# Score buffers and the down-weight quantiser of a transformer layer: one PSUM region for every query tile, and two of the quantiser's passes on ScalarE

## The reference, cut to what matters

```python
def ternary_quant(w):
    scale = jnp.mean(jnp.abs(w)) + EPS
    q = jnp.clip(jnp.round(w / scale), -1.0, 1.0) * scale
    return w + jax.lax.stop_gradient(q - w)

# attention of one head: softmax(q k^T * scale, causal) v
scores = jnp.einsum('bkgtd,bksd->bkgts', qg, k) * scale
scores = jnp.where(causal, scores, -jnp.inf)
attn = jax.nn.softmax(scores, axis=-1)

# feed-forward part, D = 2048, D_EXPERT = 8192
up = jnp.einsum('bsd,ed->bse', x, ternary_quant(W_up))
gate = jnp.einsum('bsd,ed->bse', x, ternary_quant(W_gate))
hidden = jax.nn.silu(up) * gate
out = jnp.einsum('bse,de->bsd', hidden, ternary_quant(W_down))
```

## Time and profile before

| what | us |
|---|---|
| median of 2 runs | 8734.99 |
| the 2 runs | 8610.41 and 8859.57 |
| the profiled execution | 8481.26 |
| its span on the slowest core | 8479.5 |
| its spans on the 8 cores | 8459.3 to 8479.5 |

### The profile page before, as it was taken

How to read it: one execution, slowest core, us unless ns; L and a number is a source line. 1 busy time by engine, 2 the same in 40 slices (tenths; PEclk the granted TensorE clock), 3 DMA queues, 4 the chain that set the end, 5 groups by cost and what they waited for, 6 DMA issues and landing times.

```text
span 8479.5 us, 68560 instructions; the slowest of 8 cores (8459.3 to 8479.5 us)
## 1 busy us (share of the span) xinstructions
PE 4851.5 (57%) x22987; PEld 2208.8 (26%) x22987; DVE 3210.5 (38%) x4854; ACT 1728.5 (20%) x3014; POOL 639.7 (8%) x1086
## 2 busy tenths in 40 slices
PE   1533443444444433346511149999999999587686
PEld 1111111111111111122211124444444444233232
DVE  4044424432444244312365655555555554000000
ACT  3123323332333233211111112112211111000000
POOL 0111111111111111100000000000000000000000
PEclk9855565556555655577755569999999999798898
DMA  2222222222222222242244432122121221424333
GB/s 83 32 76 85 82 43 85 82 74 51 82 77 76 57 75 77 70 100 79 75 129 127 132 114 78 75 76 84 75 77 75 78 81 48 143 85 143 94 83 88
DMA packets 279157, 709.29 MB, mean 84 GB/s; under 512 B 119488, under 2 KB 119520, under 8 KB 246688
## 3 DMA queue, kind: packets, MB, share of 16 engines
q0 software_dynamic: 157216, 350.46, 14.8%
q1 hardware_dynamic: 121600, 354.46, 12.8%
HBM read 607.32 MB, written 109.05 MB: 84 GB/s over the span
## 4 chain that ended last, share of the span: by engine, by line
PE 53%; DVE 14%; DMA 12%; ACT 9%; issue 7%; POOL 2%; another core or an unknown queue 1%; SPq 1%; DVEq 0%; ACTq 0%; POOLq 0%
PE up_ps L1239 11%; PE gt_ps L1253 10%; PE po_a L1340 5%; PE po_b L1340 5%; DMA tdT_scr<-tds 5%; PE a_ps L462 5%; PE y_ps L752 3%; PE pr_ps L879 3%; PE pt_ps L617 3%; DVE stt L660 2%; ACT slabA L1169 2%; PE a_ps L650 2%; DMA xm<-xmid_scr 2%; ACT tds L1084 2%; DVE pt_bf L625 2%
## 5 line engine op out<-in xcount | busy, mean ns | idle before, releaser
L1239 PE MATMUL up_ps<-slabB,slabA 128*128 128x512 bf16 x4096 | 974.2, 399 | 59.7 <-ACT slabA L1169 59.7
L1253 PE MATMUL gt_ps<-slabB,slabA 128*128 128x512 bf16 x4096 | 904.9, 379 | 0.0
L617 PE MATMUL pt_ps<-id_bf,b 128*128 128x128 bf16 x2176 | 292.1, 303 | 848.3 <-DVE stt L687 462.4
L462 PE MATMUL a_ps<-slabA,wcol_bf 128*128 128x512 bf16 x1536 | 389.2, 418 | 313.1 <-DMA wcol_bf<-Wq 164.4
L1239 PEld LDWEIGHTS up_ps<-slabB,slabA 128*128 128x128 bf16 x4096 | 412.8, 102 | 590.3 <-issue 162.2
L1253 PEld LDWEIGHTS gt_ps<-slabB,slabA 128*128 128x128 bf16 x4096 | 401.0, 98 | 483.1
L700 ACT ACTIVATE w<-a_ps,stt 128x1024 f32<-128x1024 f32 (+7 forms) x384 | 329.3, 861 | 909.5 <-DVE stt L687 668.5
L1078 PE MATMUL tp_ps<-id_bf,b 128*128 128x128 bf16 x1024 | 139.6, 303 | 636.6 <-DMA tdT_scr<-tds 477.3
L650 PE MATMUL a_ps<-k_bf,q_bf 128*128 128x512 bf16 (+3 forms) x640 | 259.2, 526 | 386.9 <-DVE q_bf L565 248.0
L401 ACT ACTIVATE pdump<-pw 128x1024 f32<-128x1024 f32 x384 | 404.2, 1054 | 370.1 <-DMA pw<-W_down 125.8
L617 PEld LDWEIGHTS pt_ps<-id_bf,b 128*128 128x128 bf16 x2176 | 203.4, 133 | 1021.3 <-issue 1021.3
(11 more groups left out here) (168 smaller groups left out, 6454.2 us busy)
## 6 DMA issues: line engine op xcount, KB each, us to landing
pw<-W_down POOLq DMA_DIRECT2D x128, 512.0 KB, 4.4
pw<-W_up POOLq DMA_DIRECT2D x128, 512.0 KB, 4.5
pw<-W_gate POOLq DMA_DIRECT2D x128, 512.0 KB, 4.4
wd<-W_down SPq DMA_DIRECT2D x64, 1024.0 KB, 7.1
wu<-W_up SPq DMA_DIRECT2D x64, 1024.0 KB, 5.1
wg<-W_gate SPq DMA_DIRECT2D x64, 1024.0 KB, 7.6
td<-tdT_scr SPq DMA_DIRECT2D x256, 256.0 KB, 2.7
xt<-xb SPq DMA_DIRECT2D x32, 1024.0 KB, 6.8
```

The lines of the kernel that those rows point to most:

```text
L462: lambda e, dt=dt, sub=sub, tc=tc: e.matmul(a_ps[:, sub * 512:(sub + 1) * 512], wcol_bf[:, dt * 128:(dt + 1) * 128], slabA[:, dt, tc * 512 ...
L617: e.transpose(pt_ps[:, par * 1024 + u * 128: par * 1024 + (u + 1) * 128], b1[:, jt * 128:(jt + 1) * 128], id_bf[:]), inc="t")
L1239: tc=tc, par=par: e.matmul(up_ps[:, sub * 512:(sub + 1) * 512], ttuA[par][:, dt * 128:(dt + 1) * 128], slabB[:, dt, tc * 512:(tc + 1) * 51 ...
L1253: par=par: e.matmul(gt_ps[:, tc * 512:(tc + 1) * 512], ttgA[par][:, dt * 128:(dt + 1) * 128], slabB[:, dt, tc * 512:(tc + 1) * 512], start ...
```

## The change

Two parts, with nothing in common.

**Part A, attention:** bb and bo are gone. Every query tile uses a_ps and w2 from column 0 and the same columns of stt, and the scores of tile iq (1 to 7) wait for the exponential of tile iq-1.

**Part B, quantiser of W_down:** two new pairs of buffers, awb (f32) and sgb (bf16). ScalarE computes abs(2**k * w) into awb and sign(w) into sgb. VectorE subtracts the term scl[:,4:5] from awb, compares the difference with the scale (is_gt), and multiplies the comparison by the sign into b1. SyncE's reload of wd waits for ScalarE. ScalarE waits for VectorE's use of awb and sgb two chunks before.

```diff
@@ attention, tiles of one head
-                            bb = 2 * (iq % 2) if nch <= 2 else 0
-                            bo = bb * 512
...
-                                ctx.wait("tensor", "s", exp_ch_s[bb + c])
+                                ctx.wait("tensor", "s", exp_ch_s[c])
...
-                                exp_ch_s[bb + 2 * c] = ctx.cnt["s"]
-                                if bb + 2 * c + 1 < 4:
-                                    exp_ch_s[bb + 2 * c + 1] = ctx.cnt["s"]
+                                exp_ch_s[2 * c] = ctx.cnt["s"]
+                                if 2 * c + 1 < 4:
+                                    exp_ch_s[2 * c + 1] = ctx.cnt["s"]
@@ quantiser of W_down
                     if ci >= 2:
-                        ctx.wait("sync", "v", qd_par[par])
+                        ctx.wait("sync", "s", qd_par[par])
                     ctx.dma("sync", wd[:],
                             w_down[r * 128:(r + 1) * 128, ec * 2048:(ec + 1) * 2048],
                             sem=wsm)
-                    ctx.wait("vector", wsm)
+                    ctx.wait("scalar", wsm)
                     if ci == 0:
-                        ctx.wait("vector", "v", scl_done_v)
-                    ctx.emit("vector", lambda e, wd=wd: e.tensor_scalar(
-                        w2[:], wd[:], scl[:, 60:61], None, ALU.mult), inc="v")
+                        ctx.wait("scalar", "v", scl_done_v)
+                    if ci >= 2:
+                        ctx.wait("scalar", "v", qv_par[par])
+                    ctx.emit("scalar", lambda e, wd=wd, awb=awb: e.activation(
+                        awb[:], wd[:], AF.Abs, scale=scl[:, 60:61]), inc="s")
+                    ctx.emit("scalar", lambda e, wd=wd, sgb=sgb: e.activation(
+                        sgb[:], wd[:], AF.Sign), inc="s")
+                    qd_par[par] = ctx.cnt["s"]
+                    ctx.wait("vector", "s", ctx.cnt["s"])
+                    ctx.emit("vector", lambda e, awb=awb: e.tensor_scalar(
+                        w1[:], awb[:], scl[:, 4:5], None, ALU.subtract),
+                        inc="v")
                     ctx.wait("vector", "v")
                     ctx.emit("vector", lambda e: e.tensor_scalar(
-                        w1[:], w2[:], scl[:, 4:5], None, ALU.add), inc="v")
-                    ctx.wait("vector", "v")
-                    ctx.emit("vector", lambda e, wd=wd: e.tensor_scalar(
-                        wd[:], w1[:], scl[:, 12:13], None, ALU.is_lt), inc="v")
-                    ctx.wait("vector", "v")
-                    ctx.emit("vector", lambda e: e.tensor_scalar(
-                        w1[:], w2[:], scl[:, 4:5], None, ALU.subtract), inc="v")
+                        w2[:], w1[:], scl[:, 0:1], None, ALU.is_gt), inc="v")
                     ctx.wait("vector", "v")
                     if ci >= 1:
                         ctx.wait("vector", "t", ctx.cnt["t"])
-                    ctx.emit("vector", lambda e, wd=wd: e.scalar_tensor_tensor(
-                        b1[:], w1[:], scl[:, 0:1], wd[:],
-                        ALU.is_gt, ALU.subtract), inc="v")
-                    qd_par[par] = ctx.cnt["v"]
+                    ctx.emit("vector", lambda e, sgb=sgb: e.tensor_tensor(
+                        b1[:], w2[:], sgb[:], ALU.mult), inc="v")
+                    qv_par[par] = ctx.cnt["v"]
```

More of the change, by code:

```diff
@@ L645, in build_program @@
                                 last = (c == nch - 1)
-                                ctx.wait("tensor", "s", exp_ch_s[bb + c])
+                                ctx.wait("tensor", "s", exp_ch_s[c])
                                 ctx.emit("tensor",
[L648 to L651, removed]
+                                         lambda e, c=c, n=n, last=last, iq=iq:
+                                         e.matmul(a_ps[:, c * 512:c * 512 + n],
                                                   q_bf[:, iq * 128:(iq + 1) * 128],
@@ L657, in build_program @@
                                     ctx.wait("vector", "t", ctx.cnt["t"])
-                                    ctx.emit("vector", lambda e, c=c, n=n,
-                                             bb=bb, bo=bo:
+                                    ctx.emit("vector", lambda e, c=c, n=n:
                                              e.reduce_max(
-                                                 st[:, 80 + bb + c:81 + bb + c],
-                                                 a_ps[:, bo + c * 512:
-                                                      bo + c * 512 + n],
+                                                 st[:, 80 + c:81 + c],
+                                                 a_ps[:, c * 512:c * 512 + n],
                                                  axis=AX.X, negate=True),
@@ L668, in build_program @@
                             nd_ = W - cd * 512
[L669 to L672, removed]
+                            ctx.emit("tensor", lambda e, kd=kd, cd=cd, nd_=nd_:
+                                     e.matmul(
+                                         a_ps[:, cd * 512:cd * 512 + nd_],
                                          id_bf[:],
@@ L677, in build_program @@
                             ctx.wait("vector", "t", s_done)
[L678 to L682, removed]
+                            ctx.emit("vector", lambda e, cd=cd, nd_=nd_:
+                                     e.reduce_max(
+                                         st[:, 80 + cd:81 + cd],
+                                         a_ps[:, cd * 512:cd * 512 + nd_],
                                          axis=AX.X, negate=True), inc="v")
@@ L693, in build_program @@
                             else:
-                                bias_col = st[:, 80 + bb:81 + bb]
+                                bias_col = st[:, 80:81]
                             ctx.wait("scalar", "v", ctx.cnt["v"])
@@ L698, in build_program @@
                                 n = min(1024, W - c * 1024)
[L699 to L704, removed]
+                                ctx.emit("scalar", lambda e, c=c, n=n,
+                                         bias_col=bias_col: e.activation(
+                                             w2[:, c * 1024:c * 1024 + n],
+                                             a_ps[:, c * 1024:c * 1024 + n],
                                              AF.Exp, bias=bias_col, scale=1.0,
-                                             accum_out=st[:, 88 + bb + c:
-                                                          89 + bb + c]),
+                                             accum_out=st[:, 88 + c:89 + c]),
                                          inc="s")
-                                exp_ch_s[bb + 2 * c] = ctx.cnt["s"]
-                                if bb + 2 * c + 1 < 4:
-                                    exp_ch_s[bb + 2 * c + 1] = ctx.cnt["s"]
+                                exp_ch_s[2 * c] = ctx.cnt["s"]
+                                if 2 * c + 1 < 4:
+                                    exp_ch_s[2 * c + 1] = ctx.cnt["s"]
                             exp_done = ctx.cnt["s"]
@@ L728, in build_program @@
                             else:
-                                den_col = st[:, 88 + bb:89 + bb]
+                                den_col = st[:, 88:89]
                             ctx.emit("vector", lambda e, den_col=den_col:
@@ L734, in build_program @@
                             ctx.wait("vector", "t", pt_last_t[0])
[L735 to L739, removed]
+                            ctx.emit("vector", lambda e, W=W: e.tensor_scalar(
+                                b1[:, 0:W], w2[:, 0:W], st[:, 96:97], None,
+                                ALU.mult), inc="v")
                             pend_pt[0] = (iq, ctx.cnt["v"])
@@ L1024, in build_program @@
                 tds = sb("tds", [128, 2048], BF16)
+                awb0 = sb("awb0", [128, 2048], F32)
+                awb1 = sb("awb1", [128, 2048], F32)
+                sgb0 = sb("sgb0", [128, 2048], BF16)
+                sgb1 = sb("sgb1", [128, 2048], BF16)
                 pp_ps2 = p35.enter_context(nc.psum_tensor("pp_ps2", [128, 512], F32))
@@ L1035, in build_program @@
                 qd_par = [0, 0]
+                qv_par = [0, 0]
                 for ci in range(64):
@@ L1040, in build_program @@
                     wd = (wd0, wd1)[par]
+                    awb = (awb0, awb1)[par]
+                    sgb = (sgb0, sgb1)[par]
                     wsm = ("u0", "u1")[par]
                     if ci >= 2:
-                        ctx.wait("sync", "v", qd_par[par])
+                        ctx.wait("sync", "s", qd_par[par])
                     ctx.dma("sync", wd[:],
```

10 lines of the change are left out of this document (4 added, 6 removed).

## The result

| | before | changed |
|---|---|---|
| median | 8707.07 (26 runs) | 8785.25 (27 runs) |
| profiled execution | 8481.26 | 8604.19 |
| its span, slowest core | 8479.5 | 8602.7 |
| its span, mean of 8 cores | 8469.7 | 8583.6 |

The ratio is 1.0144, with a 95% interval of 1.0107 to 1.0181: the change makes the kernel slower by 1.4%, which is within 2%. Both kernels' times spread over some 4.6% of themselves, because in part of the executions the cores of a die run at a lower granted clock; the ratio is taken of the others.

The account below looks back on a forecast made before the run. The prediction took hand-overs between engines as the bound, in the quantiser the store's landing. It summed 8481 + 94 + 1 + 3 = 8579 us for a profiled execution, plus 129 = 8708 us, range 8555 to 8880.

Parts of the forecast that it names:

- The bound of the kernel before: Quantiser: the store's landing sets the 12.14 us cycle, VectorE's passes are covered, a load beside the store costs about 2 us.
- Part B: Quantiser: ScalarE and VectorE passes become one chain behind the copies, cycle 13.58 us, costing 94 us (31 to 129).
- hand-over to TensorE: Quantiser: from the end of VectorE's multiply to the next transposes, 0.13 us a cycle.
- Table loads: ScalarE: at most one extra table load for Sign, 1.3 us.
- rival 3: Quantiser: two table loads of 1.28 us in every chunk, 164 us on top, 3.1% slower; chance 0.11.
- Part A: Attention: scores wait for the previous tile's exponential, mostly covered by ScalarE's pass over the weights; 3 us in all, 16 uncovered.
- The sign that it gave: Attention: 3152 us within 20, and waits of the scores for the exponential in tiles 1 to 3.
- The sum: Whole kernel, an execution like the profiled one: 8481 + 94 + 1 + 3 = 8579 us, 1.2% more.
- The step that failed: Whole kernel: 129 us, the lower shown run's distance above the profiled execution, added to 8579 gives 8708 us.
- Rival 1: Quantiser: multiply takes only 1.29 us and the store stays the bound, cycle 12.1 to 12.6 us; chance 0.10.
- Rival 2: Quantiser: the store with no load beside it ends the cycle at 10.0 us, 132 us less, 1.6% faster; chance 0.03.
- Rival 4: Attention: the scores' whole time lands on the chain in all seven tiles, 112 us, 2.5% slower; chance 0.06.

Follow-up runs that it names:

- e5: The kernel before, with two tds buffers used by turns for the quantiser's store: cycle 7.92 us, quantiser 263 us shorter, ratio 0.9677 to the kernel before.
- e1: The kernel before with part A alone, its quantiser unchanged: cycle 12.08 us, quantiser 1 us and attention 2 us longer than in the kernel before.
- e4: The changed kernel with Abs and Sign of the next chunk ahead of this chunk's copies in ScalarE's list: cycle 10.32 us, quantiser 111 us shorter than before the change.
- e7: The kernel before without attention's pass over the weights (loads and absolute sums left out, constants instead): attention 155 us shorter than in the kernel before.
- e8: The kernel before with part A and without attention's pass over the weights: attention 134 us shorter than in the kernel before.
- e12: The kernel before with part A alone, run again for an interval: ratio 1.0002 (0.9982 to 1.0022), cycle 12.09 us, attention 1 us longer.
- e6: The changed kernel with two tds buffers used by turns for the store: cycle 13.87 us, quantiser 113 us longer than before the change, ratio 1.0162.

## Why the prediction was right or wrong

**The bound of the kernel before** was right. The store's landing bounded the quantiser (e5: 4.2 us a cycle less when it no longer does), VectorE's passes were covered, and the load beside the store cost it 2 us (e1's 6.8 against e4's 4.9).

**Part B** was right in its mechanism and 13 us short in its size, 94 against 107. The terms, against the timeline of the changed kernel:

| term | predicted | measured |
|---|---|---|
| transposes and copies, Abs and Sign | 8.27 | 8.26 (4651.92 to 4660.18) |
| hand-over to VectorE | 0.12 | 0.11 |
| subtract and compare | 2.78 | 2.85 |
| multiply | 2.28 | 2.29 |
| hand-over to TensorE | 0.13 | 0.26 |
| cycle | 13.58 | 13.77 |

Every pass was right to 0.02 us. Short were two hand-overs. Behind the wait that ends last there stands a second one that is long satisfied (VectorE's for the transposes of the chunk before, TensorE's for the store). The first chunk of the changed kernel has neither of the two, and there TensorE follows the multiply after 0.14 us (4224.78 - 4222.35 - 2.29) where it is 0.26 in the others:

```profile
4222.35 2.29 DVE L1059 TENSOR_TENSOR b<-w,sgb 128x2048 bf16<-128x2048 f32 x1
4224.78 1.01 PE L1072 MATMUL tp_ps<-id_bf,b 128*128 128x128 bf16 x8 [10.28 <-DVE b L1059]
```

So the second wait costs 0.12 us on TensorE, and on VectorE 0.07 (0.17 idle before the multiply, against 0.10 from pass to pass in the earlier trace rows). Together that is 0.2 us a cycle, 12 us. The 0.13 us that the prediction took from the earlier trace rows (4622.38 - 4620.96 - 1.29) is not a hand-over at all: L1059 works there on the chunk after, and these transposes need L1064's result, ready since 4616.86, and the landing of the store. The profile names L1059 only because it ended last. That 0.13 is so near the 0.14 of the first chunk is luck.

**Table loads.** There are two in the changed kernel, as before, and none for Sign:

```profile
L1260 ACT ACT_TABLE_LOAD x1 | 1.3, 1283 | 9.2 <-PE up_ps L1233 9.2
```

So rival 3 didn't occur, and the 1.3 us that I had allowed for Sign weren't needed. The Trainium skill's list in "ScalarE: Activation LUTs" (section on table sets), which names copy, identity and abs as being in every set, doesn't name Sign; that Sign ran between Abs and the copies with no load shows that the set loaded here has it, and not that every set does.

**Part A** was right: 3 us foreseen; 1 to 5 measured, with an error of some 3, and a ratio of 1.0002. Its cover was the one named, as e7 and e8 show. The sign that it gave was too narrow: the scores wait for L691 in tiles 5 to 7 as well, not in tiles 1 to 3 alone.

**The sum** for an execution like the profiled one was 8579, +1.2%; the profiled one has 8604, +1.45%, inside the range given for it (8540 to 8615). Of the 25 us that are missing 13 are part B's; the remainder is that the slowest core is another one, with 20 us of its own in the last stage, where the mean of the cores changed by 1.3.

**The step that failed** is the last of the sum: from the profiled execution to a median. I added 129 us, the distance of the lower of the two runs shown, and got 8708. That is under the 8735 that stood as the median of the kernel before (and level with the 8707 of its 26 runs), so the number forecast a gain of 0.3% while the text beside it forecast a loss of 1.2%. A loss was measured, as the text had it and not as the number had it. The number ought to have kept the ratio: 8735 x 1.0115 = 8836, or the same distance as before, 8579 + 254 = 8833. That would have been 50 us above the measured 8785, and the reason for that much can be seen too: over 26 and 27 runs the medians stand 226 and 181 us above the profiled executions, so this distance is itself uncertain by some 50 us, half of what the change does. A median of such runs can't carry a change of 1%; the ratio in the section on the result, known to 0.4% either way, can.

**The rivals.** Rival 1 (a cheap multiply) fell to its 2.29 us. Rival 2 (the store gets quicker and the cycle ends at 10 us) was right about the store and wrong about the cycle; e4 comes near its price: a cycle of 10.3 us where it had 10.0, and 111 us where it had 132. Rival 4 fell to e12.

## What to carry to other kernels

An engine's busy share says nothing on what relieving it is worth: look which wait ends last, and test by giving that one a second buffer. Work moved to a less busy engine takes its place in that engine's list, and behind an instruction that closes the loop it lies on the path in full; issue it ahead of the instructions that wait for this chunk's results. And when a forecast is made from one execution, carry it over as a ratio, never by adding to one and comparing with another.

## What the runs showed of the hardware

- A wait that is already satisfied, behind the one that ends last, costs about 0.1 us: from VectorE to TensorE 0.14 us with none (first chunk of the changed kernel), 0.26 with one, 0.36 with two (e6).
- A store in pieces of 256 bytes (0.5 MB) lands after 4.8 us with no load beside it for 3.2 us (changed kernel), and after 6.8 us where a load of 1 MB is issued 1.3 us after it (e1); 3.2 us between the two keep the median at 4.9 in e4's shorter cycle.
- Multiplying an f32 tensor by a bf16 one on VectorE takes 2.29 us for 2048 columns on 128 partitions, as an f32 pair does (2.28, on 64 partitions); Abs with a pointer scale takes 2.00 and Sign 1.90 on ScalarE.
